# The decays of a gated linear attention computed in rows, and stored with ten transfers a group

## The chip, the cores and the metric

The kernel runs on one core of a Trainium2 chip. Its time is the device time of that core in microseconds (us); the kernel before takes 3340.37 us, the median of three runs (3338.11 to 3342.51). The core has a matrix engine (PE, TensorE), whose weight loads are shown apart as PEld, a vector engine (DVE), a scalar engine (ACT), a general engine (POOL, GpSimd) and a queue processor (SP, SyncE) that here issues all transfers. The engines run side by side and meet at semaphores; each executes its own instructions in the order of its program.

## The reference, cut to what matters

```python
# B = 8 batches, N = 2048 tokens, D = 256, H = 16 heads of 64
h = layernorm(x) * (1 + ca) + sa
q = elu(h @ Wq) + 1;  k = elu(h @ Wk) + 1;  v = h @ Wv
a = sigmoid(h @ Wa + ba + 2.0)                 # one decay per token and head
S = a_t * S + k_t v_t^T;  z = a_t * z + k_t    # a scan over the tokens
out = (q_t . S) / (q_t . z + 1e-6)
x = x + ga * (out @ Wo)
h = layernorm(x) * (1 + cb) + sb
x = x + gb * experts(h)                        # 8 experts, the top 2, with gates
```

The change touches only how the decays `a`, and the products of them that the scan needs, are made and stored.

## The kernel before, in words

The kernel has two phases. The first is the attention, with the output product and the residual; the second is the experts, which the change doesn't touch. The attention handles 32 groups of 512 tokens one after the other. A group is cut into four chunks of 128 tokens, each of two half chunks of 64 (eight of 64 in all), and its 16 heads are taken in eight pairs. So the loop `attention_steps` runs eight steps (u = 0 to 7) for a group. In a step every engine does one part of several pairs: PE projects K and Q for the pair three ahead (`project`, L594 to L596), multiplies queries with earlier states (L743), makes the state products (L757) and the output products (L768) of nearer pairs, transposes the finished pair (L784), does a dense job (below) and ends with the scores (L822). This order is written out by hand and is the same in all groups.

The dense jobs fill the steps: each is looked up in `DENSE_JOBS` by step and part. "v" projects values, "wo" makes the output product, "h" transposes the normalized input of the next group. Two of them serve the decays of the next group: "z" in step 2 and "a" in step 3. All small products go through PSUM bank Q, which the Q projection uses too; `q_bank_free` (L616) makes PE wait, before it projects Q in a step, until the engine that read the bank for the job before is done.

The decays take this way. In step 2 PE multiplies slices of 32 tokens of `h32` (as weights) by `wa` (16 moving columns): 32 products, which the compiled program runs as 64 instructions on tiles of 128 rows and 32 columns (L646). DVE adds the bias (L881), ACT takes exp(-z) (L544), DVE adds 1 (L888), takes the reciprocal (L891) and writes two copies into `a_cols`, one zero at the chunks' first tokens, the other zero elsewhere (L895, L896). In step 3 PE transposes `a_cols` (L656, four transposes) so that heads lie in 16 partitions and tokens in 512 columns. ACT copies the rows to `a_row` (L509), DVE runs the scan that gives the products of the decays from each chunk's start (`lam_row`, L904). PE waits for both before it projects Q in step 4 (L627, L628). SP stores five pieces of `a_row` and two of `lam_row` to DRAM at the start of step 4, waits until they have landed, and then reads them back, spread over the partitions, one pair at a time: `a_bc` (L366), from which DVE scans the decay matrix (L952), and `lam_bc` (L372), used by POOL (L447) and by the chain of states on DVE (L929).

DVE's order is the second thing to know. In a step it finishes K (L944) and Q (L946), scans the decay matrix (L952), runs the chain of states (L929, eight instructions), the job of the step, the division (L966 to L971) and the masked scores (L981). In step 2 the sigmoid's L891, L895 and L896 come behind L981, and one of the normalization's statistics (L866) behind them, before L944 of step 3. PE does not start its dense job in a step before K of that step is finished (L790). ACT copies with a scale in `kd_sb` (L554, eight instructions) at the end of a step, and L981 waits for it.

At the very start SP issues the loads one after the other: `c`, `ba` (spread over the partitions), `wa`, the first tokens, then the weights.

Of the kernel before, what the change touches and what calls it, by code (L numbers as in the profile page):

```python
# [39 lines left out]
CH = 128  # L40
# [12 lines left out]
ROWS_B = 64  # L53
# [19 lines left out]
def unit(T, u, ahead):  # L73
# [7 lines left out]
              (2, 1): ("z", 1, 0), (3, 0): ("v", 1, 1), (3, 1): ("a", 1, 0), (4, 0): ("v", 1, 2), (5, 0): ("v", 1, 3),  # L81
# [44 lines left out]
def adaln_block(nc, x, Wq, Wk, Wv, Wo, Wa, ba, gate_W, gate_b, expert_W, expert_b, c, wmod, out):  # L126
# [3 lines left out]
    rows_dram = nc.dram_tensor("rows_dram", [2, 2, PAIRS, 2, GT], F32, kind="Internal").ap()  # L130
# [14 lines left out]
def attention_phase(nc, tokens, Wq, Wk, Wv, Wo, Wa, ba, c, wmod, x1_dram, gates_dram, rows_dram, mod, ident, bank):  # L145
    with ExitStack() as ctx:
# [11 lines left out]
        wa = sb("wa", [128, KT, HEADS])  # L158
        ba_raw = sb("ba_raw", [128, HEADS])
        ba2 = sb("ba2", [128, HEADS])  # L160
# [3 lines left out]
        first = sb("chunk_first", [128, 1])  # L164
        later = sb("chunk_later", [128, 1])
# [16 lines left out]
        a_tok = sb("a_tok", [128, NCH, HEADS])  # L182
        a_sig = sb("a_sig", [128, NCH, HEADS])
        a_cols = sb("a_cols", [128, NCH, ROWS_B + HEADS])
        a_row = sb("a_row", [HEADS, GT])
        lam_row = sb("lam_row", [HEADS, GT])
# [45 lines left out]
        z_ps = sem("z_ps"); zb_ready = sem("zb_ready"); z_exp = sem("z_exp"); a_step = sem("a_step"); a_ready = sem("a_ready")  # L232
        arow_ps = sem("arow_ps"); a_row_ready = sem("a_row_ready"); lam_row_ready = sem("lam_row_ready")
# [35 lines left out]
        SMALL = 3  # L269
        MOD_A = 4  # L270
        ROW_STORES = 7
        SECTION = [0, 1, 3, 4]

# [12 lines left out]
        def _(sp):  # L286
            wm = wmod.rearrange("(k p) n -> p k n", p=128)
            sp.dma_start(c_sb, c).then_inc(small_loaded, 16)
            sp.dma_start(ba_raw[:, :], ba.partition_broadcast(128)).then_inc(small_loaded, 16)
            sp.dma_start(wa[:, :, :], Wa.rearrange("(k p) n -> p k n", p=128)).then_inc(small_loaded, 16)  # L290
# [33 lines left out]
            def store_rows(T, sT):  # L324

                dst = rows_dram[sT, 0].rearrange("q f (h t i) -> h f q t i", h=2, t=NCH)
                sp.wait_ge(a_row_ready, T + 1)
                src = [a_row[hd * PAIRS:(hd + 1) * PAIRS, :].rearrange("r (t f i) -> r t f i", f=2, i=CK) for hd in range(2)]
                sp.dma_start(dst[0, 0], src[0][:, :, 0, :]).then_inc(rows_stored, 16)
                sp.dma_start(dst[0, 1], src[0][:, :, 1, :]).then_inc(rows_stored, 16)  # L330
                sp.dma_start(dst[1, 0], src[1][:, :, 1, :]).then_inc(rows_stored, 16)
                sp.dma_start(dst[1, 1, :, 0:NCH - 1, :], src[1][:, 1:NCH, 0, :]).then_inc(rows_stored, 16)
                sp.dma_start(dst[1, 1, :, NCH - 1, :], src[1][:, 0, 0, :]).then_inc(rows_stored, 16)
                sp.wait_ge(lam_row_ready, T + 1)
                for hd in range(2):
                    sp.dma_start(rows_dram[sT, 1, :, hd, :], lam_row[hd * PAIRS:(hd + 1) * PAIRS, :]).then_inc(rows_stored, 16)
                sp.wait_ge(rows_stored, (T + 1) * 16 * ROW_STORES)
                sp.sem_inc(rows_seen)

            def step(T, place_in_batch, u):  # L340
# [14 lines left out]
                if u == 1 and exists(T + 2):  # L355
                    sp.wait_ge(xn_ready, T + 2)
                    sp.dma_start(x_in[:, :, :], tokens[bass.ds(T + 2, 1)].rearrange("g p c d -> (g p) c d"))\
                      .then_inc(x_loaded, 16)
                if u == 4 and exists(T + 1):
                    store_rows(T + 1, 1 - s)  # L360
                if exists(Tn):
                    slot = pn % 2
                    if exists(Tb):
                        sp.wait_ge(decay_ready, b + 1)
                    for half in range(2):
                        sp.dma_start(a_bc[slot][half * CK:(half + 1) * CK, :], rows_dram[sn, 0, pn, half].partition_broadcast(CK))\  # L366
                          .then_inc(a_loaded[slot], 16)
                    if exists(Tb):
                        sp.wait_ge(state_step, (b + 1) * NCK)
                        sp.wait_ge(qs_ready, b + 1)  # L370
                    for hd in range(2):
                        sp.dma_start(lam_bc[slot][hd * DH:(hd + 1) * DH, :], rows_dram[sn, 1, pn, hd].partition_broadcast(DH))\  # L372
                          .then_inc(lam_loaded[slot], 16)
# [7 lines left out]
        def _(pool):  # L381
# [17 lines left out]
            pool.memset(first[:, :], 0.0).then_inc(fills, 1)  # L399
            pool.memset(later[:, :], 1.0).then_inc(fills, 1)  # L400
            pool.memset(half_neg[:, :], -0.5).then_inc(consts_ready, 1)
            pool.wait_ge(fills, 4)
            pool.affine_select(out=ident[:, :], in_=ident[:, :], compare_op=ALU.not_equal, fill=1.0, base=0,
                               pattern=[[-1, 128]], channel_multiplier=1).then_inc(consts_ready, 1)
            for t, fill, pattern in ((eye8[:, :, :], 1.0, [[0, NCK], [-1, CK]]), (first[:, :], 1.0, [[-1, 1]]), (later[:, :], 0.0, [[-1, 1]])):
                pool.affine_select(out=t, in_=t, compare_op=ALU.not_equal, fill=fill, base=0, pattern=pattern,
                                   channel_multiplier=1).then_inc(fills, 1)
            pool.wait_ge(fills, 7)
            for t, fill, pattern in ((eye8[:, :, :], 1.0, [[0, NCK], [-1, CK]]), (first[:, :], 1.0, [[-1, 1]]), (later[:, :], 0.0, [[-1, 1]])):
                pool.affine_select(out=t, in_=t, compare_op=ALU.not_equal, fill=fill, base=-CK, pattern=pattern,  # L410
                                   channel_multiplier=1).then_inc(consts_ready, 1)
            pool.wait_ge(consts_ready, 4)
            pool.tensor_copy(eye, eye8[:, 0, :]).then_inc(eye_ready, 1)
            reciprocal_deviation(0)
            ln_apply(0, range(NCH))

# [51 lines left out]
        def _(act):  # L468
# [31 lines left out]
            def dense_out(T, s, u, part):  # L500
# [5 lines left out]
                if job == "a":  # L506
                    act.wait_ge(arow_ps, of + 1)
                    after(act, rows_stored, of * 16 * ROW_STORES)
                    act.activation(a_row[:, :], Q[0:HEADS, :], ACT.Copy).then_inc(a_row_ready, 1)  # L509
# [7 lines left out]
            def step(T, place_in_batch, u):  # L517
# [24 lines left out]
                if u == 2 and exists(T + 1):  # L542
                    act.wait_ge(zb_ready, T + 2)
                    act.activation(a_tok[:, :, :], a_tok[:, :, :], ACT.Exp, scale=-1.0).then_inc(z_exp, 1)  # L544
# [17 lines left out]
        def _(pe):  # L562

            pe.wait_ge(consts_ready, 5)
# [51 lines left out]
            def q_bank_free(T, u):  # L616
# [23 lines left out]
            def z_job(T):  # L640
                pe.wait_ge(h32_ready, T * 2 + 2)
                for ch in range(NCH):
                    for kt in range(KT):

                        for at in range(0, CH, SLICE):
                            mm = pe.matmul(Q[at:at + SLICE, ch * HEADS:(ch + 1) * HEADS],  # L646
                                           h32[:, kt, ch * CH + at:ch * CH + at + SLICE],
                                           wa[:, kt, :].rearrange("p (q h) -> p h q", h=2),
                                           start=(kt == 0), stop=(kt == KT - 1))
                mm.then_inc(z_ps, 1)  # L650

            def arow_job(T):
                pe.wait_ge(a_ready, T + 1)
                pe.wait_ge(zb_ready, T + 1)
                for ch in range(NCH):
                    mm = pe.transpose(Q[0:ROWS_B + HEADS, ch * CH:(ch + 1) * CH], a_cols[:, ch, :], ident[:, :])  # L656
                mm.then_inc(arow_ps, 1)
# [36 lines left out]
            def dense_job(T, s, u, part):  # L694
# [9 lines left out]
                if job == "a":  # L704
                    arow_job(of)
# [123 lines left out]
        def _(dve):  # L829
# [7 lines left out]
            dve.tensor_scalar(ba2[:, :].rearrange("p (h q) -> p q h", h=2), ba_raw[:, :].rearrange("p (q h) -> p q h", h=2),  # L837
                              DECAY_BIAS_SHIFT, None, ALU.add).then_inc(ba_ready, 1)
# [4 lines left out]
            dve.wait_ge(consts_ready, 5)  # L843
            dve.memset(a_cols[:, :, :], 0.0)
# [33 lines left out]
            def z_out(T):  # L878
                dve.wait_ge(z_ps, T + 1)
                dve.wait_ge(ba_ready, 1)  # L880
                dve.tensor_tensor(a_tok[:, :, :], Q[:, 0:NCH * HEADS].rearrange("p (c h) -> p c h", h=HEADS),  # L881
                                  ba2[:, :].unsqueeze(1).to_broadcast([128, NCH, HEADS]), ALU.add).then_inc(zb_ready, 1)

            def sigmoid_step(T, k):

                if k == 0:
                    dve.wait_ge(z_exp, T + 1)
                    dve.tensor_scalar(a_tok[:, :, :], a_tok[:, :, :], 1.0, None, ALU.add).then_inc(a_step, 1)  # L888
                if k == 1:
                    dve.wait_ge(a_step, T * 2 + 1)  # L890
                    dve.reciprocal(a_sig[:, :, :], a_tok[:, :, :]).then_inc(a_step, 1)  # L891
                if k == 2:
                    after(dve, arow_ps, T)
                    dve.wait_ge(a_step, T * 2 + 2)
# [574 lines left out]
```

## Time and profile before

| what | before |
|---|---|
| median of three runs | 3340.37 us |
| the profiled execution, time | 3338.53 us |
| its span, first to last instruction | 3336.8 us |
| PE busy | 3224.1 us, 97% |
| DVE busy | 2442.7 us, 73% |
| ACT busy | 1815.1 us, 54% |
| POOL busy | 1434.8 us, 43% |
| mean granted TensorE clock | 0.991 |

The span is 1.7 us shorter than the time of the same execution. The engines overlap, so their busy times don't add up; what counts is which engine is the one that others don't wait for. Matmuls are pipelined in the profile: one starts before the one ahead has ended, so the distance from start to start says what one costs, not its duration.

### The profile page before, as it was taken

The page shows a single profiled execution, that of the slowest core. Times are in us where ns is not written, and L with a number is a line of the kernel's source. Part 1 is how long each engine was busy: PE and PEld are TensorE (multiplying, and loading weights), DVE is VectorE, ACT ScalarE, POOL GpSimd, SP SyncE. Part 2 cuts the span into 40 slices and gives each one's busy share as a digit, 9 for nine tenths or more (in the row PEclk, how much of TensorE's full clock was granted, in tenths as well). Part 3 has the DMA queues.
Part 4 walks back from the last instruction along what each step waited for, and adds up shares of the span by engine and source line. Part 5 has one row for each costly group of instructions (what it writes and reads, how often), then busy time and mean ns, then how long its engine had stood idle before and what let it go on. Part 6 is the DMA issues. An engine that isn't in the chain of part 4 may idle for free. (4 is left out here: it accounts for less than half of the span.)

```text
span 3336.8 us, 128741 instructions
## 1 busy us (share of the span) xinstructions
PE 3224.1 (97%) x50858; PEld 2737.6 (82%) x50858; DVE 2442.7 (73%) x6617; ACT 1815.1 (54%) x4492; POOL 1434.8 (43%) x1117
## 2 busy tenths in 40 slices
PE   7999999999999999999999999999977999999999
PEld 6888888888888888888888888888865888878887
DVE  6777777777777777777777777777746787878786
ACT  5666666666666666666666666666632322222221
POOL 4444445545544454455455444444431222222222
PEclk9999999999999999999999999999997999999999
DMA  4222222222232222222222322222212111111110
GB/s 151 79 74 77 81 79 79 79 73 76 84 90 79 77 78 78 79 79 79 73 76 81 93 79 76 77 79 79 73 49 77 52 39 39 52 39 39 52 39 26
DMA packets 158608, 238.66 MB, mean 72 GB/s; under 512 B 30216, under 2 KB 82488, under 8 KB 157752
## 3 DMA queue, kind: packets, MB, share of 16 engines
q1 hardware_dynamic: 158008, 230.33, 21.9%
q8 instruction: 417, 6.83, 0.8%
q14 instruction: 183, 1.50, 0.1%
HBM read 194.58 MB, written 35.67 MB: 69 GB/s over the span
## 5 line engine op out<-in xcount | busy, mean ns | idle before, releaser
L447 POOL TENSOR_TENSOR qs_sb<-lam_bc,qk_sb 128x512 f32<-128x512 f32 x256 | 532.7, 2081 | 1069.0 <-DVE qk_sb L946 966.3
L554 ACT ACTIVATE kd_sb<-bank_scores,decay 128x64 f32<-128x64 f32 x2048 | 447.9, 330 | 285.4 <-PE bank_scores L822 276.1
L929 DVE SCALAR_TENSOR_TENSOR s_mid<-s_mid,lam_bc,bank_dense 128x65 f32<-128x65 f32 x1536 | 433.4, 282 | 54.8
L455 POOL TENSOR_TENSOR oT_lo<-oT,oT_hi 128x512 fp32r<-128x512 f32 x256 | 328.4, 1283 | 77.7 <-ACT oT_hi L531 77.7
L513 ACT ACTIVATE qk_sb<-bank 128x512 f32<-128x512 f32 x512 | 317.3, 620 | 52.5 <-PE bank L596 36.8
L1141 POOL TENSOR_TENSOR acc<-acc,gb 128x512 f32<-128x512 f32 x64 | 83.1, 1299 | 581.3 <-DVE acc L1313 558.2
L515 ACT ACTIVATE qk_sb<-qk_sb 128x512 f32<-128x512 f32 x512 | 323.3, 631 | 16.3
L981 DVE TENSOR_TENSOR p_sb<-bank_scores,decay 128x512 f32<-128x512 f32 x256 | 176.6, 690 | 202.2 <-ACT kd_sb L554 199.5
L952 DVE TENSOR_TENSOR_SCAN decay<-a_bc,eye 128x512 f32<-128x512 f32 x256 | 310.8, 1214 | 2.7 <-DMA a_bc<-rows_dram 2.4
L594 PE MATMUL bank<-wv_hi,h_hi 128*128 128x256 f32 x1024 | 306.8, 300 | 4.8 <-DVE qk_sb L944 4.1
L1313 DVE SCALAR_TENSOR_TENSOR acc<-bank,comb,acc 128x256 f32<-128x256 f32 x512 | 229.7, 475 | 105.6 <-ACT acc L1181 96.3
L822 PE MATMUL bank_scores<-qk_sb 64*64 64x128 f32 x8192 | 284.9, 275 | 8.6 <-ACT oT_hi L531 4.3
L689 PE MATMUL bank<-wo_hi,oT_hi 128*128 128x256 f32 x1024 | 290.7, 284 | 1.4 <-DVE xo L860 0.8
L595 PE MATMUL bank<-wv_lo,h_hi 128*128 128x256 f32 x1024 | 287.8, 281 | 1.6 <-issue 1.6
L596 PE MATMUL bank<-wv_hi,h_lo 128*128 128x256 f32 x1024 | 288.3, 282 | 1.0 <-issue 1.0
L691 PE MATMUL bank<-wo_hi,oT_lo 128*128 128x256 f32 x1024 | 288.0, 281 | 0.0
L690 PE MATMUL bank<-wo_lo,oT_hi 128*128 128x256 f32 x1024 | 287.8, 281 | 0.0
L946 DVE SCALAR_TENSOR_TENSOR qk_sb<-bank,qk_sb 128x512 f32<-128x512 f32 x256 | 176.7, 690 | 124.5 <-ACT qk_sb L515 123.1
L822 PEld LDWEIGHTS bank_scores<-qk_sb 64*64 64x64 f32 x8192 | 225.4, 132 | 48.5 <-issue 35.7
L1313 DVE SCALAR_TENSOR_TENSOR acc<-bank_scores,comb,acc 128x256 f32<-128x256 f32 x512 | 231.3, 476 | 43.8 <-PE bank_scores L1227 42.8
L530 ACT ACTIVATE oT<-bank_scores 128x512 f32<-128x512 f32 x224 | 134.2, 599 | 209.5 <-PE bank_scores L784 209.5
L594 PE MATMUL bank<-h_hi,wk_hi 128*128 128x512 f32 x512 | 227.8, 445 | 14.1 <-ACT oT_hi L531 10.0
(198 smaller groups left out, 8561.4 us busy)
## 6 DMA issues: line engine op xcount, KB each, us to landing
a_bc<-rows_dram SPq DMA_DIRECT2D x512, 128.0 KB, 3.1
lam_bc<-rows_dram SPq DMA_DIRECT2D x512, 128.0 KB
x_in<-in_L_attn_x_dram SPq DMA_DIRECT2D x32, 512.0 KB, 6.0
x_res<-in_L_attn_x_dram SPq DMA_DIRECT2D x32, 512.0 KB, 4.1
x_dram<-x_res SPq DMA_DIRECT2D x32, 512.0 KB, 2.9
x<-x_dram SPq DMA_DIRECT2D x32, 512.0 KB, 3.3
out_dram<-x SPq DMA_DIRECT2D x32, 512.0 KB, 3.0
ew_raw<-in_L_ffn_expert_W_dram SPq DMA_DIRECT2D x8, 256.0 KB, 5.6
```

What stands on the lines that cost most here:

```text
L447: pool.tensor_tensor(qs_sb[:, na, :], lam_bc[na][:, :], q_sb, ALU.mult).then_inc(qs_ready, 1)
L455: pool.tensor_tensor(oT_lo[:, u, :], oT32[:, :], oT_hi[:, u, :].bitcast(F32), ALU.subtract).then_inc(oT_lo_ready, 1)
L513: act.activation(t, x[:, :], ACT.Relu, scale=-1.0).then_inc(x_neg, 1)
L515: act.activation(t, t, ACT.Exp, scale=-1.0).then_inc(x_exp, 1)
L554: ins = act.activation(kd_sb[:, t, hd * DH:(hd + 1) * DH], KTR[:, hd, t * CK:(t + 1) * CK], ACT.Copy, scale=decay[:, hd, t, CK - 1:CK])
L594: pe.matmul(dst, s_hi, m_hi, start=(n == 0), stop=False)
L596: mm = pe.matmul(dst, s_lo, m_hi, start=False, stop=(n == last))
L689: pe.matmul(dst, oT_hi[:, pt, tok], wo_hi[:, pt, :], start=(pt == 0 and i == 0), stop=False)
L822: mm = pe.matmul(KTR_S[rows[half], hd, :, t, :], k_sb[rows[hd], ch * CK:(ch + 1) * CK], eye_q[rows[hd], :, :], start=True, stop=True)
L929: dve.scalar_tensor_tensor(dst, src, lam_bc[nb][:, (ch + 1) * CK - 1:(ch + 1) * CK], U[ch], ALU.mult, ALU.add).then_inc(state_step, 1)
L952: dve.tensor_tensor_scan(decay[:, :, :, :].rearrange("p h t i -> p (h t i)"), a_bc[na][:, :], eye8[:, :, :].rearrange("p c i -> p (c i)"), ...
L1313: dve.scalar_tensor_tensor(a, y[:, (k // 2) * D:(k // 2 + 1) * D], comb[s % 2][:, 2 * pair + i, e:e + 1], a, ALU.mult, ALU.add).then_inc(y ...
```

## The change

The two decay jobs become one. `wa` is now the weight matrix, with each head's column doubled (REP = 2, so 32 columns), and the tokens are the moving operand: a quarter of the group's tokens at a time, 128 columns, into one of four blocks of 32 partitions. The result lies in rows from the start: partition = quarter x head x copy, 128 tokens in columns. PE's "a" job and its transposes are gone, with ACT's and DVE's copies of them. The bias is one scalar per partition, used in ACT's exp. DVE does all the rest (`decay_rows`) at the end of step 2, on tiles of 128 partitions and 128 columns.

```diff
-              (2, 1): ("z", 1, 0), (3, 0): ("v", 1, 1), (3, 1): ("a", 1, 0), (4, 0): ("v", 1, 2), (5, 0): ("v", 1, 3),
+              (2, 1): ("z", 1, 0), (3, 0): ("v", 1, 1), (4, 0): ("v", 1, 2), (5, 0): ("v", 1, 3),
 # PE
-                for ch in range(NCH):
-                    for kt in range(KT):
-                        for at in range(0, CH, SLICE):
-                            mm = pe.matmul(Q[at:at + SLICE, ch * HEADS:(ch + 1) * HEADS],
-                                           h32[:, kt, ch * CH + at:ch * CH + at + SLICE],
-                                           wa[:, kt, :].rearrange("p (q h) -> p h q", h=2), ...
+                for kt in range(KT):
+                    h_tok = h32[:, kt, :].rearrange("p (t f i) -> p t f i", t=NCH, f=2)
+                    for f in range(2):
+                        for th in range(2):
+                            at = quarter(f, th)
+                            mm = pe.matmul(Q[at:at + REP * HEADS, 0:GT // 4]..., wa[:, kt, :],
+                                           h_tok[:, 2 * th:2 * th + 2, f, :], start=(kt == 0), stop=(kt == KT - 1))
-            def arow_job(T):
-                ...
 # what PE waits for before it projects Q
                 if u == 3 and exists(T + 1):
-                    pe.wait_ge(zb_ready, T + 2)
-                if u == 4 and exists(T + 1):
-                    pe.wait_ge(a_row_ready, T + 2)
-                    pe.wait_ge(lam_row_ready, T + 2)
+                    pe.wait_ge(z_exp, T + 2)
 # ACT, in step 2 behind the copy of the values (L544 and L509 are gone)
+                if job == "z":
+                    act.wait_ge(z_ps, of + 1)
+                    act.activation(a_exp[:, :], Q[:, 0:GT // 4], ACT.Exp, bias=neg_ba[:, 0:1], scale=-1.0).then_inc(z_exp, 1)
 # DVE, in step 2 behind L981 (L881, L888, L891, L895, L896 and L904 are gone)
+            def decay_rows(T):
+                firsts = [t[:, :].rearrange("p (t i) -> p t i", t=2)[:, :, 0:1] for t in (a_first, a_rows)]
+                dve.wait_ge(z_exp, T + 1)
+                dve.tensor_scalar(a_exp[:, :], a_exp[:, :], 1.0, None, ALU.add).then_inc(a_step, 1)
+                ...
+                dve.reciprocal(a_rows[:, :], a_exp[:, :]).then_inc(a_step, 1)
+                ...
+                dve.tensor_copy(firsts[0], firsts[1]).then_inc(a_step, 1)
+                dve.memset(firsts[1], 0.0).then_inc(a_row_ready, 1)
+                dve.tensor_tensor_scan(lam_rows[:, :], a_rows[:, :], a_first[:, :], 0.0, ALU.mult, ALU.add)...
 # SP: six stores of a_rows and four of lam_rows, in step 3; the wait for them stays in step 4
+                if u == 3 and exists(T + 1):
+                    store_rows(T + 1, 1 - s)
                 if u == 4 and exists(T + 1):
-                    store_rows(T + 1, 1 - s)
+                    sp.wait_ge(rows_stored, (T + 2) * 16 * ROW_STORES)
+                    sp.sem_inc(rows_seen)
 # SP, at the start: the bias one column at a time, ahead of wa and of the first tokens
-            sp.dma_start(ba_raw[:, :], ba.partition_broadcast(128)).then_inc(small_loaded, 16)
+            for at in range(0, 128, REP * HEADS):
+                for r in range(REP):
+                    sp.dma_start(ba_raw[at + r:at + REP * HEADS - 1 + r:REP, :], ba.rearrange("(h o) -> h o", o=1))\
+                      .then_inc(small_loaded, 16)
```

The six stores of `a_rows` move 16 or 8 rows of 512 or 256 bytes each; the four of `lam_rows` move 16 rows as two pieces of 256 bytes. The loads of `a_bc` and `lam_bc` keep their number and size; only the order of the rows in DRAM differs. On POOL two of the start's constants go and one copy, which doubles `wa`, is added.

## Rows read from the trace of the kernel before

**Rows 1.** Windows view, the attention: busy us of each engine and its instructions, clock.
```profile
33.90:2462.60 2428.70, 2376.78 (x44660) 2044.81 (x44660) 1767.59 (x4334) 1576.78 (x4059) 1200.40 (x848) 1.00 0.26 79
```

**Rows 2.** Timeline of PE, end of a step 2: start, us, line, tiles, count.
```profile
1537.28 0.28 PE L596 MATMUL bank<-wv_hi,h_lo 128*128 128x256 f32 x1
1537.49 0.73 PE L646 MATMUL bank<-wa,h 128*32 128x16 f32 x64
1538.30 1.10 PE L822 MATMUL bank_scores<-qk_sb 64*64 64x128 f32 x32
```

**Rows 3.** Timeline of PE, steps 3 and 4 of the same group.
```profile
1544.49 0.36 PE L594 MATMUL bank<-wv_hi,h_hi 128*128 128x256 f32 x1
...
1545.88 0.28 PE L596 MATMUL bank<-wv_hi,h_lo 128*128 128x256 f32 x1
1546.00 0.60 PE L656 MATMUL bank<-ident,a_cols 128*80 128x128 f32 x4
1546.53 1.10 PE L822 MATMUL bank_scores<-qk_sb 64*64 64x128 f32 x32
...
1548.60 0.40 PE L595 MATMUL bank<-h_lo,wk_hi 128*128 128x512 f32 x1
1548.84 0.39 PE L596 MATMUL bank<-h_hi,wk_lo 128*128 128x512 f32 x1
1549.77 0.47 PE L594 MATMUL bank<-h_hi,wq_hi 128*128 128x512 f32 x1 [0.54 <-DVE lam_row L904]
1550.07 0.40 PE L595 MATMUL bank<-h_lo,wq_hi 128*128 128x512 f32 x1
...
1554.73 0.28 PE L596 MATMUL bank<-wv_hi,h_lo 128*128 128x256 f32 x1
1555.01 1.10 PE L822 MATMUL bank_scores<-qk_sb 64*64 64x128 f32 x32
```

**Rows 4.** Timeline of ACT in the same group, end of step 2 and of step 3.
```profile
1539.72 0.26 ACT L544 ACTIVATE a_tok<-a_tok 128x64 f32<-128x64 f32 x1 [1.53 <-DVE a_tok L881]
1539.88 1.73 ACT L554 ACTIVATE kd_sb<-bank_scores,decay 128x64 f32<-128x64 f32 x8
...
1547.75 1.75 ACT L554 ACTIVATE kd_sb<-bank_scores,decay 128x64 f32<-128x64 f32 x8 [0.44 <-PE bank_scores L822]
```

**Rows 5.** Timeline of DVE in the same group, steps 2 to 4.
```profile
1541.72 0.69 DVE L981 TENSOR_TENSOR p_sb<-bank_scores,decay 128x512 f32<-128x512 f32 x1 [0.90 <-ACT kd_sb L554]
1542.33 0.54 DVE L891 RECIPROCAL a_sig<-a_tok 128x64 f32<-128x64 f32 x1
...
1543.23 0.42 DVE L866 BATCH_NORM_STATS2 stats<-x_in 128x6 f32<-128x256 f32 x1
1543.57 0.67 DVE L944 SCALAR_TENSOR_TENSOR qk_sb<-bank,qk_sb 128x512 f32<-128x512 f32 x1
...
1548.40 1.22 DVE L904 TENSOR_TENSOR_SCAN lam_row<-a_row,bank 16x512 f32<-16x512 f32 x1
...
1553.40 1.21 DVE L952 TENSOR_TENSOR_SCAN decay<-a_bc,eye 128x512 f32<-128x512 f32 x1
```

**Rows 6.** One line of the code at the start: count, ns min/median/max, when, form.
```profile
L834 DVE RECIPROCAL h<-h x1: 1741/1741/1741, 5.1 to 5.1; 8x256 f32<-8x256 f32 x1
```

**Rows 7.** Timeline of SP in step 4, and the page's DMA part (KB, us to landing).
```profile
1549.53 0.49 SPq L329 DMA_DIRECT2D rows_dram<-a_row  x1
1550.06 0.31 SPq L330 DMA_DIRECT2D rows_dram<-a_row  x1
...
a_bc<-rows_dram SPq DMA_DIRECT2D x512, 128.0 KB, 3.1
```

**Rows 8.** Timeline of the start: SP, DVE and PE.
```profile
1.30 0.37 SPq L289 DMA_DIRECT2D ba_raw<-in_L_attn_ba_dram  x1
2.19 0.47 SPq L291 DMA_DIRECT2D x_in<-in_L_attn_x_dram  x1
...
35.80 0.43 DVE L866 BATCH_NORM_STATS2 stats<-x_in 128x6 f32<-128x256 f32 x1 [4.80 <-DMA x_in<-in_L_attn_x_dram]
...
37.62 0.47 PE L594 MATMUL bank<-h_hi,wq_hi 128*128 128x512 f32 x1 [2.07 <-DVE lam_row L904]
```

**Rows 9.** Waits view, whole trace: us in total, times, longest.
```profile
PE bank L594 <- DVE lam_row L904: 17.4, 31, 2.1
```

More of the change, by code:

```diff
@@ L52 @@
 LO = 32
-ROWS_B = 64
+REP = 2
 def after(eng, sem, count):
@@ L181, in attention_phase @@
         v_sb = sb("v_sb", [128, NCH, HEADS, VW])
[L182 to L186, printed above, removed]
+        a_exp = sb("a_exp", [128, GT // 4])
+        a_rows = sb("a_rows", [128, GT // 4])
+        a_first = sb("a_first", [128, GT // 4])
+        lam_rows = sb("lam_rows", [128, GT // 4])
         a_bc = [sb(f"a_bc{i}", [128, GT]) for i in range(2)]
@@ L398, in _ @@
             pool.memset(eye8[:, :, :], 0.0).then_inc(fills, 1)
[L399 to L400 removed]
             pool.memset(half_neg[:, :], -0.5).then_inc(consts_ready, 1)
[L402 removed]
+            pool.wait_ge(fills, 2)
             pool.affine_select(out=ident[:, :], in_=ident[:, :], compare_op=ALU.not_equal, fill=1.0, base=0,
                                pattern=[[-1, 128]], channel_multiplier=1).then_inc(consts_ready, 1)
[L405 to L412, printed above, removed]
+            pool.affine_select(out=eye8[:, :, :], in_=eye8[:, :, :], compare_op=ALU.not_equal, fill=1.0, base=0,
+                               pattern=[[0, NCK], [-1, CK]], channel_multiplier=1).then_inc(fills, 1)
+            pool.wait_ge(fills, 3)
+            pool.affine_select(out=eye8[:, :, :], in_=eye8[:, :, :], compare_op=ALU.not_equal, fill=1.0, base=-CK,
+                               pattern=[[0, NCK], [-1, CK]], channel_multiplier=1).then_inc(consts_ready, 1)
+            pool.wait_ge(consts_ready, 3)
             pool.tensor_copy(eye, eye8[:, 0, :]).then_inc(eye_ready, 1)
@@ L505, in dense_out @@
                     h_out(of, so)
[L506 to L509, printed above, removed]
+                if job == "z":
+                    act.wait_ge(z_ps, of + 1)
+                    act.wait_ge(ba_ready, 1)
+                    after(act, a_step, of * 3)
+                    act.activation(a_exp[:, :], Q[:, 0:GT // 4], ACT.Exp, bias=neg_ba[:, 0:1], scale=-1.0).then_inc(z_exp, 1)
             def exp_of_negative(a, x, t, x_ps, x_neg, x_exp):
@@ L876, in ln_variance @@
                    .then_inc(var_ready, 1)
[L878 to L894, printed above, removed]
-                    dve.tensor_scalar(a_cols[:, :, 0:HEADS], a_sig[:, :, :], later[:, 0:1], None, ALU.mult)
-                    dve.tensor_scalar(a_cols[:, :, ROWS_B:ROWS_B + HEADS], a_sig[:, :, :], first[:, 0:1], None, ALU.mult)\
-                       .then_inc(a_ready, 1)
@@ L903, in decay_products @@
                 dve.wait_ge(a_row_ready, T + 1)
-                dve.tensor_tensor_scan(lam_row[:, :], a_row[:, :], Q[ROWS_B:ROWS_B + HEADS, :], 0.0,
-                                       ALU.mult, ALU.add).then_inc(lam_row_ready, 1)
+                dve.tensor_tensor_scan(lam_rows[:, :], a_rows[:, :], a_first[:, :], 0.0, ALU.mult, ALU.add).then_inc(lam_row_ready, 1)
             def dense_out(T, s, u, part):
```

95 lines of the change are left out of this document (44 added, 51 removed).

## The prediction
> **What bounds the kernel now.** I read the busy shares first, stage by stage. In the attention PE is busy 2376.8 of 2428.7 us at full clock, DVE 1767.6 and ACT 1576.8 [rows 1]. So PE sets the time, and the other engines count only where PE waits for them. Next I read PE's timeline in one ordinary group, looking for where its stream of starts is broken by the decays' work, and then the other engines' timelines only around those places. Three places come out.
>
> In step 2 the last value product starts at 1537.28, the z job at 1537.49, the scores at 1538.30 [rows 2]: 1.02 us. In step 4, with no decay job, the same passage (1554.73 to 1555.01) is 0.28 [rows 3]. The z job costs PE 0.74 us.
>
> In step 3 the passage with four transposes is 1545.88 to 1546.53 [rows 3], 0.65 us: the a job costs 0.37.
>
> In step 4 PE's next start after 1548.84 is 1549.77 and the next again 1550.07 [rows 3]. Two starts of that kind lie 0.24 apart, so the wait for the row scan takes 0.69 and restarting another 0.06 (0.30 against 0.24): 0.75 us. The waits view counts only idle behind the pipeline's end, and still has 31 such waits with 17.4 us [rows 9], one in each group.
>
> Together 1.86 us of a group, by 31 groups 58 us. That is the most that could go; the z job comes back in another form.
>
> **The change, part by part.**
>
> *The z job on PE.* 64 instructions with 16 moving columns become 16 with 128 (eight products, each two instructions, as the 32 before were 64). The trace has no such form. What one costs alone I take from the transposes: four in 0.60 us at a duration of 0.27 [rows 3] (I take one duration as the last start to the end), so (0.60 - 0.27)/3 = 0.11 us from start to start with 128 columns. If four tiles work side by side, it is a quarter: the scores, 128 columns on four tiles of 64x64, are 32 in 1.10, so (1.10 - 0.27)/31 = 0.027 us each [rows 3]. The old job's (0.73 - 0.18)/63 = 0.009 us each [rows 2] doesn't decide it, its columns are too few. From the old last start (1537.49 + 0.73 - 0.18 = 1538.04) to the scores was 0.26; the new matmul is 0.09 longer, so 0.35. The entry stays 0.21. Side by side: 0.21 + 15 x 0.027 + 0.35 = 0.96 against 1.02, a gain of 0.06. One after the other: 0.21 + 1.65 + 0.35 = 2.21, a loss of 1.19. Two at once: 0.21 + 0.82 + 0.35 = 1.38, a loss of 0.36. I take the first, since the scores show exactly four in flight, with two column tiles reading different data from the same rows; what differs is 128 rows for each tile instead of 64.
>
> The row of the scores shows that four tiles give the whole factor of 4 (0.11/0.027) [rows 3]. The Trainium skill, "TensorE: Matmul & The Clock Gate", part "Packing small matmuls", states less for column tiles: 2.38 for three, and 3.07 for four row tiles. By 3.07 the 15 intervals would be 0.54 instead of 0.41, the z job 0.13 dearer a group, and the sum 4 us smaller.
>
> *ACT in step 2.* L544 goes. It waited 1.53 us for DVE, and held up the kd copies (1539.88) [rows 4]. In step 3, with nothing in front, the copies start 1.22 us after the scores (1546.53 to 1547.75) [rows 3, 4]; in step 2 that would be 1539.52. The new exp reads PSUM behind the value copy and is over before the scores are, if it costs less than the 1.3 us for which ACT is free there (from 1539.72 - 1.53 on). So the kd copies, and with them L981, which follows them, start 0.36 earlier, and by the z job's 0.06 more: L981 at 1541.30 instead of 1541.72.
>
> *DVE in step 2: the new critical piece.* Behind L981 come today 0.90 us (L891 at 1542.33 to L866 at 1543.23) [rows 5]. That is 0.54 for the reciprocal and 0.18 for each of two small ones. In their place: add 1 on 128 columns, about 0.21; the reciprocal, 0.54 for 64 columns and 1.74 for 256 [rows 5, 6], so 6.2 ns a column and 0.94 for 128; copy and memset of two columns, some 0.12 and 0.10; the scan, 1.21 for 512 columns [rows 5], so near 0.34 for 128; and about 0.03 at each of four waits of DVE for itself, less 0.08 of overlap at the end: 1.75 us. That is 0.85 more (between 0.6, if fixed parts are smaller, and 1.3, if each wait for itself costs 0.1 more and the small ones 0.2). Net, L944 starts at 1543.57 - 0.42 + 0.85 = 1544.00 instead of 1543.57.
>
> PE's dense job in step 3 waits for L944: it started at 1544.49, 0.25 after L944's end at 1544.24 [rows 3, 5]. It moves to 1544.92, 0.43 later. So the z gain is absorbed and PE waits some 0.5 us here that it hardly waited before. In sum up to this point -0.43 us.
>
> *The a job.* It goes whole: +0.37. What the scores of step 3 then wait for is Q (L946), which follows L944 within 1.3 us and has the value products' 1.4 us as cover.
>
> *The wait in step 4.* The row scan (1.22 us, 1548.40 [rows 5]) no longer stands between PE and the Q projection; the bank is freed by ACT's exp a step earlier. +0.75. What is late next is the division on DVE, behind the same chain; it moves 0.8 us earlier (1.22 less 0.43), the same as PE or more, and so doesn't take the wait's place.
>
> *Stores on SP.* Ten instead of seven, 0.49 for the first and 0.31 plus 0.04 for others [rows 7], some 3.6 us, from about 1543.4 (when a_rows is ready) to 1547. Queued behind are the loads of a_bc for pair 7 (1.2 us to issue, 3.1 to land [rows 7]): landed by about 1551.3. DVE needs them at L952 in step 4, 1553.40 less 0.7 [rows 5]; 1.4 us of cover. lam_bc waits for the chain of step 3 anyway. If the cover were gone, DVE's scan would be late first, and PE only through it. Moved from step 4, the store's landing time no longer delays the next group's first loads. I cost all of it at 0, between 0 and +0.5 us a group lost.
>
> *The start.* Eight loads of the bias instead of one stand ahead of everything: 7 x 0.45 (0.37 and the gap to the next) = 3.1 us [rows 8]. The first products, which wait for these loads, go 3.1 later. On the other side PE's 2.07 for the first row scan goes [rows 8]. DVE however waits at 35.80 for x_in, whose load also comes later. I take 2 us lost, between 0 and 4.
>
> **The sum.** A group: -0.43 + 0.37 + 0.75 = 0.69 us gained; 31 groups 21.4; less 2.0: 19.4 us. On the profiled execution, 3338.5 - 19.4 = 3319.1. The median of the runs is 1.8 above that execution, so 3321.0 for it. With the ends: DVE's 0.6 gives 7.8 us more gain, its 1.3 gives 14 less.
>
> **The rivals.**
>
> *R1, the quarters run one after the other.* Each tile streams 128 rows; if the array or the memory gives one stream at a time, the z job loses 1.19 instead of gaining 0.06. L981 and L944 shift with the scores, so nothing hides it: 0.69 - 1.25 = -0.56 a group, 17 us, with the start 19 us slower: 3360. It turns the sign from 0.07 us from start to start on: 0.027, plus the group's 0.63 (0.69 less its share of the start, 2/31) over 15 intervals. For it: the form with 128 rows and long moving operands is nowhere in the trace. Against: the scores, and the old z job, whose starts come 0.009 us apart in the same tile form. Two at once (0.69 - 0.42 = 0.27 a group) gives 8.4 - 2 = 6 us faster, 3334.
>
> *R2, DVE takes back nearly all.* decay_rows costs 1.5 to 2 us more than L891 to L896, as strided writes of one column or self-waits are slow; then L944 is a further 0.65 or more late and PE waits for it in step 3: 3321 + 20 = 3341 at 0.65, no change. For it: PE already starts 0.25 after L944, so every ns counts. Against: the 0.90 us of today hold two operations of 64 columns beside the reciprocal's 0.54, 0.18 each.
>
> *R3, more is gained.* The chain of DVE work costs only what hides, PE starts its dense job in step 3 when it does now, the start loses nothing: 0.06 + 0.37 + 0.75 + 0 = 1.18 a group, 36 us: 3304. Against: the reciprocal's slope is plain in two rows.
>
> *R4, given back on PE.* Each group is entered earlier, and the states' chain, the reload of a_bc and lam_bc or the residual's transfers keep their own pace; a wait of PE for them in steps 5 to 1 gives half of the 21.4 back: 3332. For it: their slack is not on PE's rows. Against: PE idles only 52 us in 2429 now [rows 1], 17.4 of them in the wait that goes, so that little else is near to binding.
>
> **How the numbers follow.** Forecast 56%, R1 7%, two at once 7%, R2 11%, R3 9%, R4 10%. A measurement tells about 0.2% (6.7 us) from no change. Faster by more: the forecast, R3, R4 and half of two at once, less what the forecast's own low edge leaves out: 76%. Same: 15%. Slower: 9%. The range reaches from 3308 (DVE's price at its lower end, nothing lost at the start) to 3335 (two at once, R4, DVE's upper end).
>
> **What would show it.** Right: L646's line with 16 instructions a group within about 0.67 us; no line for L656 and L904's scan at 0.3 us; PE's wait for lam_row gone; a new wait of PE for K's L944 in step 3 of every group, 0.4 to 0.6 us; steps 3 and 4 together 1.1 less 0.4 shorter. Wrong: L646's block of 1.9 us (R1), L944 starting more than 1 us later after L981 than I have it (R2), no wait for L944 (R3), or a wait of PE for DVE or ACT in steps 4 to 1 that was not there (R4).

## The result and the profile after

The changed kernel takes 3349.69 us, the median of 16 runs (3341.78 to 3352.82), against 3341.91 for the kernel before (16 runs, 3337.39 to 3349.43, among them the three shown ahead). The ratio is 1.0017 with a 95% interval of 1.0010 to 1.0024: slower by 0.17%, inside the 0.2% that I called no change, and outside the forecast range of 3308 to 3335. The profiled execution agrees: its span is 3347.5 us, 10.7 longer than before.

From the profile's page of the changed kernel:

```profile
PE 3205.9 (96%) x49194; PEld 2721.2 (81%) x49194; DVE 2415.9 (72%) x6585; ACT 1807.6 (54%) x4460; POOL 1400.2 (42%) x1112
```

The windows view of its attention, which answers to [rows 1]:

```profile
36.60:2473.50 2436.90, 2358.22 (x43049) 2027.90 (x43049) 1741.23 (x4302) 1569.69 (x4028) 1166.01 (x848) 1.00 0.26 79
```

PE has 1600 fewer instructions there and 19 us less work (2376.8 to 2358.2), and yet the stretch is 8 us longer. So PE idles 79 us instead of 52: 27 us of new waiting. The attention also starts 2.7 us later (36.60 against 33.90). Together that is the 10.7; what follows the attention has not changed.

A step runs from the start of one K projection on PE to the start of the next. Their lengths say where the waiting is (us, median over the groups, 32 of them and 31 for step 4, means in brackets):

| step | before | after | forecast of the difference |
|---|---|---|---|
| 2 | 8.46 (8.51) | 8.18 (8.17) | -0.06 |
| 3 | 8.21 (8.23) | 8.40 (8.40) | +0.12 |
| 4 | 8.48 (8.47) | 7.72 (7.72) | -0.75 |
| 5 | 7.72 (7.86) | 8.70 (9.09) | 0 |

The other four steps differ by 0.13 at most. Steps 2 to 4 give 0.85 us a group (0.92 by the means), more than the 0.69 forecast. Step 5, where nothing was changed, takes 0.98 more in the median and 1.23 in the mean. Its very first one lies in the start, which is treated below; without it the mean is 1.19, 37 us for 31 groups.

The timeline of PE in one group of the changed kernel, end of step 2 to step 5, answers to [rows 2, 3] (start, us, line, tiles, count, idle before):

```profile
1544.19 0.28 PE L605 MATMUL bank<-wv_hi,h_lo 128*128 128x256 f32 x1
1544.39 0.64 PE L655 MATMUL bank<-h,wa 128*32 128x128 f32 x16
1544.97 1.10 PE L820 MATMUL bank_scores<-qk_sb 64*64 64x128 f32 x32
...
1548.67 0.40 PE L605 MATMUL bank<-h_hi,wq_lo 128*128 128x512 f32 x1
1548.99 0.28 PE L741 MATMUL bank_nums<-carry,qs_sb 64*64 64x65 f32 x2
...
1551.80 0.36 PE L603 MATMUL bank<-wv_hi,h_hi 128*128 128x256 f32 x1 [0.55 <-DVE qk_sb L924]
...
1564.79 0.40 PE L605 MATMUL bank<-h_hi,wq_lo 128*128 128x512 f32 x1
1565.99 0.28 PE L741 MATMUL bank_nums<-carry,qs_sb 64*64 64x65 f32 x2 [0.80 <-issue]
```

Two rows near the end of a step are to be compared: the last Q projection and the first small product. In step 3 they start 0.32 apart, in step 5 1.20. This 0.88 is the loss of this group. The row says "issue", which is time with no releaser in the profile; in other groups the same wait is put down to DVE's division, as the waits view shows (us in total, times, longest), with other waits to read beside it:

```profile
POOL qs_sb L458 <- DMA lam_bc<-rows_dram: 410.8, 75, 19.3
...
DVE decay L932 <- DMA a_bc<-rows_dram: 43.7, 33, 2.2
...
PE bank L603 <- DVE qk_sb L924: 21.7, 31, 4.8
...
PE bank_nums L741 <- DVE o_sb L951: 13.2, 12, 2.2
...
PE bank_nums L741 <- issue: 9.3, 16, 1.2
```

Before, DVE's wait for a_bc stood at 2.4 us, 3 times, POOL's for lam_bc at 102.7 us, 15 times, and PE's wait for the division at 4.2 us, twice. The wait for lam_row [rows 9] is gone. These two waits of PE at L741 (22.5 us together) are not the whole loss of step 5. Its stretch from the Q projection to the first small product (L741) grew by 20 us over 31 groups. The other 17 of the 37 lie behind it, 7 of them between the scores and the next K projection, as pauses and stretched blocks of small products for which the profile names no releaser. The timeline of DVE in the same group follows the chain (it answers to [rows 5]):

```profile
1548.04 0.69 DVE L959 TENSOR_TENSOR p_sb<-bank_scores,decay 128x512 f32<-128x512 f32 x1 [0.51 <-ACT kd_sb L563]
1548.65 0.22 DVE L879 TENSOR_SCALAR a_exp<-a_exp 128x128 f32<-128x128 f32 x1
1548.90 0.95 DVE L882 RECIPROCAL a_rows<-a_exp 128x128 f32<-128x128 f32 x1
...
1550.22 0.43 DVE L889 TENSOR_TENSOR_SCAN lam_rows<-a_rows,a_first 128x128 f32<-128x128 f32 x1
1550.56 0.40 DVE L863 BATCH_NORM_STATS2 stats<-x_in 128x6 f32<-128x256 f32 x1
1550.88 0.68 DVE L924 SCALAR_TENSOR_TENSOR qk_sb<-bank,qk_sb 128x512 f32<-128x512 f32 x1
...
1561.22 1.23 DVE L932 TENSOR_TENSOR_SCAN decay<-a_bc,eye 128x512 f32<-128x512 f32 x1 [1.67 <-DMA a_bc<-rows_dram]
...
1565.20 0.69 DVE L951 TENSOR_TENSOR o_sb<-bank_nums,rden 128x512 f32<-128x512 f32 x1
```

And the timeline of SP, the queue whose work I had costed at nothing (it answers to [rows 7]; the count is at the end of each row, durations are of all of them together):

```profile
1550.21 1.16 SPq L336 DMA_DIRECT2D rows_dram<-a_rows  x2
...
1552.45 0.69 SPq L339 DMA_DIRECT2D rows_dram<-a_rows  x1
1553.18 0.65 SPq L340 DMA_DIRECT2D rows_dram<-a_rows  x1
1553.87 3.00 SPq L345 DMA_DIRECT2D rows_dram<-lam_rows  x4
1557.00 1.15 SPq L377 DMA_DIRECT2D a_bc<-rows_dram  x2
```

The forecast's group lies 6.91 us earlier (1537.28 in [rows 2] is 1544.19 here). Shifted so, it said: stores from 1550.3 to 1553.9, a_bc landed at 1558.2, wanted at 1559.6. The stores begin at 1550.21, but last until 1557.00, 3.1 us longer; with 1.15 to issue and the 3.1 to land of [rows 7], a_bc lands at 1561.25. DVE's scan starts at 1561.22, after 1.67 us of waiting. (This group is among the worse ones: from the first store to the next load it takes 6.8 us, the median is 6.32, and DVE's 33 waits have a mean of 1.3.)

The scan, the states' chain, the division and PE's next small products follow one another. PE feels a part of DVE's delay only, because the division was ready early. In the kernel before, from the K projection of step 5 on (rows of both engines, in order of time):

```profile
1556.05 0.50 PE L594 MATMUL bank<-h_hi,wk_hi 128*128 128x512 f32 x1
...
1557.42 0.69 DVE L971 TENSOR_TENSOR o_sb<-bank_nums,rden 128x512 f32<-128x512 f32 x1
...
1559.05 0.27 PE L743 MATMUL bank_nums<-carry,qs_sb 64*64 64x65 f32 x2
```

The division ends 2.06 after the start of the step and PE takes the small product at 3.00: 0.94 of cover. In the changed kernel the step starts at 1562.12, the division ends at 1565.89, which is 3.77 after it, and PE starts 0.10 behind: 0.88 of DVE's 1.67 is left.

The start (SP first, then PE), which answers to [rows 8]:

```profile
1.23 5.05 SPq L293 DMA_DIRECT2D ba_raw<-in_L_attn_ba_dram  x8
6.96 0.46 SPq L296 DMA_DIRECT2D x_in<-in_L_attn_x_dram  x1
...
36.58 0.48 PE L603 MATMUL bank<-h_hi,wk_hi 128*128 128x512 f32 x1 [0.78 <-ACT v_sb L496]
44.45 0.58 PE L603 MATMUL bank<-wv_hi,h_hi 128*128 128x256 f32 x1 [4.83 <-DVE qk_sb L924]
```

The eight loads of the bias take 5.05 us, and x_in is issued 4.8 later. The first K projection is 2.7 later than before (33.92), the second 5.1 (43.81 to 48.92). PE's wait for DVE before the first value product is 4.83 us, where it was 1.90. From there to the end of the attention 5.7 us more are lost.

### The profile page after: what moved, and what is told of

The parts are those of the page before. It is cut to its first block and busy times, and to the rows that moved or that the text cites. A ratio compares the mean times of both kernels' runs of the same rounds, so it can differ in the third digit from the quotient of the medians.

```text
span 3347.5 us, 125416 instructions
## 1 busy us (share of the span) xinstructions
PE 3205.9 (96%) x49194; PEld 2721.2 (81%) x49194; DVE 2415.9 (72%) x6585; ACT 1807.6 (54%) x4460; POOL 1400.2 (42%) x1112
## 5 line engine op out<-in xcount | busy, mean ns | idle before, releaser
L458 POOL TENSOR_TENSOR qs_sb<-lam_bc,qk_sb 128x512 f32<-128x512 f32 x256 | 497.6, 1944 | 1108.7 <-DVE qk_sb L926 667.6
```

The source lines that it names most:

```text
L458: pool.tensor_tensor(qs_sb[:, na, :], lam_bc[na][:, :], q_sb, ALU.mult).then_inc(qs_ready, 1)
```

## The experiments

In the diffs, lines in brackets or with "..." are shortened. The theory, A: the ten stores keep SP so long that the a_bc loads queued behind them are late, and this alone costs step 5 its 1 us. The rivals: B, the same instructions would lose it wherever the stores stand, since PE or the memory pays in another way; C, the start is what costs; D, PE's loss comes from where its instructions lie in the program, which the new code has shifted.

### The a_bc loads ahead of the stores

```diff
-                if u == 3 and exists(T + 1):
-                    store_rows(T + 1, 1 - s)
...
+                    # behind the a_bc loads of the step
+                    if u == 3 and exists(T + 1):
+                        store_rows(T + 1, 1 - s)
```

> In step 3 SP now issues the two loads of a_bc for pair 7 before the ten stores; nothing else differs from the changed kernel. Theory S (the stores hold SP's queue for 6.7 us, pair 7's a_bc lands 1 to 2 us after DVE could scan it in step 4, DVE's division comes late and PE waits in step 5): DVE's wait for a_bc (43.7 us in 33 times) falls to about 3, step 5 falls from 8.7 us to 7.7, about 25 to 35 us less: 3315 to 3325. Rival M (the same stores and loads slow each other on the DMA engines, whatever their order): 3345 to 3352. Rival F (PE's pauses within a block of small products, up to 2.5 us, while instructions are loaded, are most of the loss and depend on where the code lies): only the median of step 5 falls, some 10 to 20 us less: 3330 to 3340.

Measured: 3318.73 us (3316.24 to 3321.67), 0.9925 of the kernel before (0.9908 to 0.9941). The same stores at the same prices, in another order on one queue, are worth 31 us against the changed kernel's 3349.69. SP's timeline of this kernel in one group:

```profile
1529.92 1.17 SPq L377 DMA_DIRECT2D a_bc<-rows_dram  x2
1532.41 1.16 SPq L336 DMA_DIRECT2D rows_dram<-a_rows  x2
...
1536.07 3.10 SPq L345 DMA_DIRECT2D rows_dram<-lam_rows  x4
1539.36 1.12 SPq L386 DMA_DIRECT2D lam_bc<-rows_dram  x2
```

The loads now start 2.5 us before the first store, which has to wait for a_rows anyway. DVE's wait for a_bc is 2.5 us, 3 times; step 5 is 7.72 again, and steps 2 to 4 keep their gain (8.18, 8.40, 7.72). A holds; B falls, and C as the main cause. So does a rival that the list leaves out, that the late loads of lam_bc cost PE the time: here they are still behind the stores and POOL still waits for them (273.9 us, 48 times), and step 5 is back.

The time lies 2 us below the forecast's 3321, but not by its terms. Added up over all steps, steps 2 to 4 give 27.6 us (21.4 forecast with the rest of the group at 0), the second K projection comes 4.3 later than before (2.0 forecast), step 5 behind it takes 4.7, and the four other steps give 2.9. That is 21.5 us at the end of the attention; the spans differ by 21.1 (3336.8 to 3315.7).

### The stores in step 4, where they were before

```diff
+                if u == 4 and exists(T + 1):
+                    store_rows(T + 1, 1 - s)
                 # then the wait for their landing, as before
```

> The ten stores stand at the start of step 4 again, where the seven stood in the kernel before. Theory S: pair 7's a_bc is early again and step 5 is 7.7 us, but the ten take 6.7 us and 3 to land before the first loads of the next group, which come at the earliest 10 us after step 4's begin on SP and so 1 to 2 us late for DVE in step 5: the wait moves to step 6, of 0.5 to 1.5 us; 3325 to 3345, slower than the order of e1. Rival M (contention): about the changed kernel's 3349. If the position alone were at fault: 3320, as fast as e1.

Measured: 3351.57 us (3343.81 to 3365.31), ratio 1.0026 (1.0013 to 1.0039). Waits and SP's timeline of this kernel:

```profile
DVE decay L931 <- DMA a_bc<-rows_dram: 50.4, 34, 3.0
...
PE bank_nums L740 <- DVE o_sb L950: 23.8, 17, 2.2
```

```profile
1561.30 1.16 SPq L336 DMA_DIRECT2D rows_dram<-a_rows  x2
...
1568.85 1.12 SPq L376 DMA_DIRECT2D a_bc<-rows_dram  x2
```

Ten stores at the old place delay the loads of step 4, which wait for the landing too (7.99 us from first store to next load in the median of the last 31, 3.89 before), and the loss moves one step on: step 5 is 7.72, step 6 is 8.66. Step 6 was expected to lose 0.5 to 1.5 us and loses 0.96 in the median, 1.2 in the mean. The time is above the upper end of the expectation even so, by 7 us: 31 times 1.2 are 37 us, and from the first experiment's 3319 to my 3345 there was room for 26. The mechanism of A holds at a second place.

### The bias loaded behind the weights

```diff
-        SMALL = 1 + 4 * REP + 1
+        SMALL = 2
...
-  (the eight loads of ba_raw ahead of x_in, on small_loaded)
+  (the same eight behind load_weight(WQ, Wq), on ba_loaded)
+            dve.wait_ge(ba_loaded, 16 * 4 * REP)
```

> The eight loads of the bias are issued behind the weights' loads with a semaphore of their own; else the changed kernel. Theory: the eight stood 5.05 us on SP ahead of everything, the first K projection comes 2.7 us and the second 5.1 us late; that comes back: 4 to 5 us less, 3345. Rival (the start's stores of rows and x_in set it): within 1 us of the changed kernel.

Measured: 3345.68 us (3342.60 to 3350.84), ratio 1.0006 (0.9996 to 1.0015), 4.0 us below the changed kernel by the medians and 6.5 by the spans (3341.0 and 3347.5); the interval of the ratio overlaps the changed kernel's (1.0010 to 1.0024), so the size is not sharp. The first K projection of this kernel:

```profile
31.88 0.48 PE L603 MATMUL bank<-h_hi,wk_hi 128*128 128x512 f32 x1 [0.78 <-ACT v_sb L496]
```

That is 4.7 earlier than in the changed kernel, and the second one, at 44.00, is 4.9 earlier. It is also 2.0 earlier than before, of which 0.50 are x_in's issue (1.69 against 2.19 [rows 8]). For the rest this row of the kernel before offers itself, a wait that went with the a job; its share wasn't tested:

```profile
31.11 0.61 PE L656 MATMUL bank<-ident,a_cols 128*80 128x128 f32 x4 [2.07 <-DVE a_cols L896]
```

C is real, at some 4 to 5 us, and it adds to A: step 5 stays at 8.60.

### Sigmoid ahead of the masked scores

On top of the first experiment, add 1 and the reciprocal move ahead of p_sb, into the time in which DVE waits for the kd copies (0.51 us in the group above):

```diff
+            def decay_sigmoid(T):
+                ...  # wait for exp, add 1, reciprocal: the head of decay_rows
...
+                if u == 2 and exists(T + 1):
+                    decay_sigmoid(T + 1)
                 # p_sb = bank_scores * decay, then the rest of decay_rows
```

> As e1, and DVE adds 1 and takes the reciprocal ahead of L959 (the masked scores) in step 2, in the time in which it waits for ACT. Theory: K of step 3 is finished 0.5 us earlier, PE's 0.55 us wait before the value products of step 3 goes in every group: 12 to 17 us less than e1, 3300 to 3310. Rival: L959, now 0.7 us later, holds up PE's transposes or the next scores instead; then no gain over e1.

Measured: 3302.01 us (3299.41 to 3304.16), ratio 0.9871 (0.9855 to 0.9887). DVE's timeline of this kernel in one group:

```profile
1521.02 0.22 DVE L880 TENSOR_SCALAR a_exp<-a_exp 128x128 f32<-128x128 f32 x1
1521.27 0.95 DVE L883 RECIPROCAL a_rows<-a_exp 128x128 f32<-128x128 f32 x1
1522.14 0.63 DVE L966 TENSOR_TENSOR p_sb<-bank_scores,decay 128x512 f32<-128x512 f32 x1
...
1523.66 0.67 DVE L929 SCALAR_TENSOR_TENSOR qk_sb<-bank,qk_sb 128x512 f32<-128x512 f32 x1
```

and PE's wait for K:

```profile
PE bank L605 <- DVE qk_sb L929: 4.7, 3, 4.0
```

K starts 1.52 us after p_sb, where it was 2.84 in the changed kernel. PE's wait for it falls from 21.4 us, 31 times (first experiment) to 4.7, 3 times, and step 3 from 8.40 to 7.71. So the wait that the forecast put into step 3 is there, caused as it said, and is worth 16.7 us by the medians of the two experiments and 13.7 by their spans: step 3 gives 19, and step 5 takes 3 of it back.

### Both orders and the later bias loads

```diff
+  store_rows behind the a_bc loads      (first experiment)
+  decay_sigmoid ahead of p_sb           (fourth)
+  the bias loads on ba_loaded           (third)
```

> e4's order and early reciprocal with e3's start. The three theories add up: e4 (3302) less the start's 4 to 5 us = 3297 to 3298. If the start's gain is eaten by something that both share (the first x_in load, the rows' stores), 3302.

Measured: 3294.76 us (3291.92 to 3299.61), ratio 0.9853 (0.9837 to 0.9870). It is the fastest version, 47 us below the kernel before (3341.89 in these runs). The step over the fourth experiment is 7 us by the medians and 4.6 by the spans (3302.0 and 3297.4), against the 4 us of the third experiment; the two intervals overlap a little, so its size is not sharp.

### One store of lam instead of four

```diff
-        ROW_STORES = 10
+        ROW_STORES = 7
...
+                sp.dma_start(lam_flat, lam_rows[0:127:REP, :]).then_inc(rows_stored, 16)
-                ...  # the four stores of lam_rows
```

> The changed kernel with its order on SP, but the four stores of lam_rows are one of 64 rows of 512 bytes (every second partition), which holds the same bytes in another order: seven stores, and what is read back as lam_bc is not the decays' products. Theory S: the stores take 6.7 - 3.0 + about 0.7 = 4.4 us, pair 7's a_bc lands 2.3 us earlier, before DVE wants it (it was 1.67 late in the group looked at); step 5 is 7.7 us, 3318 to 3325, though the stores still stand ahead of the loads. If their mere place in front, or the wait for lam_rows, were at fault: 3345 to 3350.

Measured: 3317.67 us (3313.99 to 3321.35), ratio 0.9925 (0.9908 to 0.9941). This version stores the rows of lam in another order, so its output is not right; it is for the time alone. The stores still stand ahead of the loads, but take 4.24 us instead of 6.32 (median from the first store to the next load); DVE's wait for a_bc is 4.3 us, 8 times. The one store of 64 rows:

```profile
L343 SPq DMA_DIRECT2D rows_dram<-lam_rows x32: 490/494/509, 38.4 to 2368.6; - x32
```

(count, ns min/median/max, when). Its four quarters cost 0.59 each, so here 64 rows cost no more than 16; the destination changed with it, from pieces of 256 bytes to rows of 512. That agrees with A from another side: what counts is the time on SP ahead of the loads.

### Stores from neighbouring partitions

```diff
-  a_rows[at:at + 61:4, :]     lam_rows[at:at + REP * HEADS - 1:REP, :]
+  a_rows[at:at + 16, :]       lam_rows[at:at + HEADS, :]
```

and so in every store. The rows stored are not the right ones; this version too is for the time alone.

> The changed kernel with all ten stores in their places and sizes, but each takes neighbouring partitions instead of every fourth or every second one (so what is stored is not the right rows). It asks why ten stores took 6.7 us of SP where I had 3.6. Theory P (an issue with a stride over partitions costs SP 0.47 to 0.75 us, one without 0.3, as the seven before): each falls to 0.30 to 0.35, the ten to 3.5, pair 7's a_bc is in time, 3318 to 3325. Rival Q (the price is that of the number of rows and pieces, 16 rows instead of 8): prices stay at 0.47 to 0.75, 3345 to 3350.

Measured: 3314.11 us (3311.52 to 3318.81), ratio 0.9917 (0.9901 to 0.9934). One line of the code each, first of the changed kernel, then of this one (count, ns min/median/max, when):

```profile
L345 SPq DMA_DIRECT2D rows_dram<-lam_rows x128: 587/594/1771, 38.6 to 2396.9; - x128
L336 SPq DMA_DIRECT2D rows_dram<-a_rows x64: 522/554/610, 35.0 to 2391.9; - x64
...
L339 SPq DMA_DIRECT2D rows_dram<-a_rows x32: 676/683/697, 37.2 to 2393.6; - x32
L340 SPq DMA_DIRECT2D rows_dram<-a_rows x32: 629/647/647, 38.0 to 2394.3; - x32
```

```profile
L345 SPq DMA_DIRECT2D rows_dram<-lam_rows x128: 320/423/1765, 38.7 to 2364.2; - x128
L336 SPq DMA_DIRECT2D rows_dram<-a_rows x64: 593/624/704, 35.3 to 2360.2; - x64
...
L339 SPq DMA_DIRECT2D rows_dram<-a_rows x32: 429/430/448, 37.9 to 2362.1; - x32
L340 SPq DMA_DIRECT2D rows_dram<-a_rows x32: 287/293/300, 38.4 to 2362.5; - x32
```

Six of the ten stores become cheaper (L339, L340, L345), four dearer (L336; L337 and L338 too, 475 to 567). Neither theory of the price was right: it hangs on the partitions' distance, but not on that alone. Ten stores cost 1.1 us less (5.23 against 6.32), and this was enough: DVE waits for a_bc 8.4 us, 15 times, at most 1.2, and step 5 is 7.72 in the median. In the groups where DVE waited 0.6 to 0.8 us, step 5 stayed 7.72; in the two where it waited 0.94 and 1.06, the division ended 3.12 and 3.16 after the start of the step and step 5 took 7.92 and 7.95. So the wait at L741 begins as an edge, when the division's 0.94 of cover is used up, and not in proportion.

### Instructions shifted on PE

On top of the first experiment:

```diff
+            for _pad in range(96): pe.sem_inc(padded)
             attention_steps(pe, step)
```

> e1 with 96 instructions on PE ahead of the attention that only count up a semaphore nobody waits for: every later instruction of PE lies 96 places further on, the work is the same. It asks how much of the pauses inside blocks of small products (2 us each at 127, 274 and 2378 us in e1) is a matter of where the code lies. If so, these pauses move or change in number, and the time differs from e1's 3319 by more than the 3 us that 96 such instructions cost, up to 10 either way; if they belong to the traffic at those times, they stay and the time is 3319 to 3322.

Measured: 3320.77 us (3315.20 to 3324.09), ratio 0.9928 (0.9912 to 0.9945). The 96 increments took far more than the 3 us expected, a figure that no row stood behind; the waits view of this kernel has them as one pause:

```profile
PE bank L645 <- issue: 9.7, 1, 9.7
```

The attention starts 8.3 us later (44.5 against 36.2), 86 ns for each. Steps are the same in their medians. PE's pauses of 1 to 2.5 us without a releaser before the output products (L768) now stand at other places: in the first experiment at 127.1, 274.1, 2301.6 and 2378.1, here at 119.3, 197.9, 633.2, 1540.0, 1715.4 and 2399.2. In the fourth experiment, whose PE code is that of the first, they are at 127.1, 273.2, 2288.1 and 2364.5, in the same groups as in the first. A longer one before a K or value product stays (3.5 us at 1271.3 and 1277.0). The median is 2 us above the first experiment's, the profiled span 6.2 (3321.9 and 3315.7). So the pauses before L768 seem to hang on where the code lies, as D has it, though with one trace of each kernel that isn't shown; moving them doesn't bring the loss of step 5 back (its median stays 7.72). Why the whole is less than 8 us longer with a start 8 us later, this run doesn't tell.

## Why the prediction was wrong

**The step that failed** is "Stores on SP. Ten instead of seven, 0.49 for the first and 0.31 plus 0.04 for others, some 3.6 us", with "1.4 us of cover" and "I cost all of it at 0, between 0 and +0.5 us a group lost". The ten took 6.8 us in the group shown (1550.21 to 1557.00), 0.68 each with the gaps, and 6.32 in the median of all groups, 0.63 each. I carried the old stores' price [rows 7] over to a form that is in none of its rows: sources of 8 or 16 rows, two or four partitions apart, instead of 8 neighbouring ones. No row shows such a store, so the upper end should have been a price above the nearest row's. That the form makes the price is not shown: with neighbouring partitions the ten still took 5.23 us. At 0.68 each the 1.4 us of cover are gone and a_bc is 1.67 us late; I had named what would follow ("DVE's scan would be late first, and PE only through it") and not priced it. Step 5 lost 0.98 us a group in the median, 1.19 in the mean, which is 30 to 37 us. That this goes with the late a_bc is shown by the experiments that make it early in three ways (first, sixth and seventh). How it reaches PE is shown for 20 us of it, the wait for the division; for the other 17 it stays open.

**What was lost** was thus R4's mechanism, "the reload of a_bc" in a step after 4, which I gave 10% and half of the gain; it took more than all of it. The argument against it, that PE idled only 52 us before and little else is near to binding, was of no use: idle time tells which waits bind, not how much room the hidden ones have left (1.4 us for DVE and 0.94 more for PE). Whether a queue has room has to be read on the queue.

**The z job** gained more: four tiles do work side by side (16 starts over 0.64 - 0.27 = 0.37 us, 0.025 apart), as the main case had it, which took 0.027. The exit was 0.21 (1544.76 to 1544.97) instead of 0.35. The whole passage is 0.78 against 0.96 forecast. R1 and two at once are out. R1 stood on blocks of 1.9 us; this one takes 0.64.

**DVE's chain** was 1.91 us (1548.65 to 1550.56) against 1.75. L944's successor starts at 1550.88; with the 6.91 the forecast said 1550.91. PE's dense job starts at 1551.80, the forecast said 1551.83. The 0.16 of price was paid by the better z job. The chain cost 1.01 more than the 0.90 that it replaced; R2 needed 1.5 to 2 more. R3 had this chain hidden altogether. The fourth experiment comes near to that and takes 3302, against R3's 3304; that the two agree is in part luck, since R3 has nothing lost at the start, and there the second K projection came 5.2 us late.

**The a job and the wait in step 4**: step 3 changed by +0.19 (forecast +0.12), step 4 by -0.76 (-0.75). Step 2 gave 0.28 instead of 0.06. Nothing took the place of the wait in step 4 itself.

**The start** lost 5 us, not 2: the eight loads took 5.05 us, 0.63 each where I had 0.45 from the one load and its gap [rows 8], and PE then waited 2.9 us longer for DVE before its first value product, which the forecast had only as "DVE however waits at 35.80". My upper end was 4.

Added up over all groups, steps 2 to 4 give 28.6 us, the start takes 5.1, step 5 takes 36.9 and the four other steps give 2.4: 11 us slower, and the attention ends 10.8 later. So the sum closes, and nothing but step 5 is needed for the changed sign. With 0 in its place it would be 26 us faster, where 19.4 was forecast. One end of the range was not what its words say: DVE's lower price and nothing lost at the start give 3321 - 7.8 - 2.0 = 3311, not 3308; nothing hangs on it.

## What to carry to other kernels

Before adding issues to a queue, write out the queue in time from the moment at which its first operand is ready: what stands behind, when that was needed, and how much room is left if each new issue costs twice what a similar one does (here 0.63 came for 0.35). If there is less room than that, put whatever has a consumer sooner ahead of them; here that change of order was worth 31 us and left the stores as they were. An engine that waits for another shortly before a chain is the place for the head of a new chain: moving two operations ahead of p_sb gave 14 to 17 us more.

## What the hardware did that I had not expected

- Issuing one store from SP took 0.29 to 0.69 us. From 16 partitions four apart it was 0.48 to 0.55, from 8 four apart 0.65 to 0.68, from 16 two apart 0.59; from neighbouring partitions the same three were 0.57 to 0.62, 0.29 to 0.43, and 0.42. One store of 64 rows two apart took 0.49. The seven stores before, of 8 neighbouring rows, had 0.30 to 0.49 in their medians. What makes the price stays open.
- Eight loads of 16 values to 16 partitions two apart took 0.63 us each, the single one that broadcast them to 128 partitions 0.37 [rows 8].
- 96 semaphore increments by themselves on PE's queue put its next work off by 8.3 us, 86 ns each.
- Products of 128 rows and 128 moving columns on four column tiles of 32, with different moving operands, started 0.025 us apart, where the transposes of 128 columns, one tile at a time, were 0.11 apart: a factor of 4.4, so four at a time.
